# First context's keys and values of a cross attention, computed at the end of the stage before and left in PSUM

## The reference, cut to what matters

```python
x = x + _L1_ffn_ref(_layernorm(x), ...)              # stage 5: 8 experts, top 2, and a shared one
x = x + _L2_xattn_ref(_layernorm(x), ctx, ctx, ...)  # stage 6

def _L2_xattn_ref(Q, K, V, Wq, bq, Wk, bk, Wv, bv, Wo, bo):
    q = (Q @ Wq + bq) / T          # 16 heads of 16
    k = K @ Wk + bk                # K = V = the context
    v = V @ Wv + bv
    attn = softmax(einsum(q, k))
    return einsum(attn, v) @ Wo + bo
```

## Time and profile before

| | us |
|---|---|
| median of 3 runs | 1916.7 (1915.62 to 1917.58) |
| the profiled execution, its own time | 1916.3 |
| its span, first to last instruction | 1914.5 |
| TensorE busy | 1792.7 (94%) |
| VectorE busy | 1049.4 (55%) |
| ScalarE busy | 847.6 (44%) |
| GpSimd busy | 555.5 (29%) |
| mean granted TensorE clock | 0.979 |

### The profile page before, as it was taken

One profiled execution on the slowest core, in us unless ns is written; L12 is line 12 of the kernel. 1 busy time (PEld: TensorE's weight loads), 2 busy tenths in 40 slices (PEclk: granted clock), 3 DMA queues, 4 the chain that ended last, 5 costly groups with the idle time before them and its releaser, 6 DMA issues.

```text
span 1914.5 us, 42986 instructions
## 1 busy us (share of the span) xinstructions
PE 1792.7 (94%) x16790; PEld 1384.6 (72%) x16790; DVE 1049.4 (55%) x2665; ACT 847.6 (44%) x2411; POOL 555.5 (29%) x596
## 2 busy tenths in 40 slices
PE   8999889999999989899999989999799899998998
PEld 6886569844766756699999967777544577766787
DVE  7787752252366438875555545556755555447411
ACT  6664541232266344334333335555511566635332
POOL 4441133100254203301222113332202465514242
PEclk9999889999999999999999999999999999998899
DMA  4221069570124110051899642111011455300397
GB/s 150 53 62 43 13 243 324 192 237 29 26 49 121 37 56 3 25 202 64 306 330 335 246 135 85 48 50 60 4 56 60 111 155 154 100 1 2 125 347 251
DMA packets 88303, 234.02 MB, mean 122 GB/s; under 512 B 10176, under 2 KB 45664, under 8 KB 81600
## 3 DMA queue, kind: packets, MB, share of 16 engines
q1 hardware_dynamic: 78416, 210.61, 33.0%
q0 software_dynamic: 5664, 15.47, 2.5%
q10 hardware_dynamic: 4048, 5.52, 0.9%
HBM read 216.35 MB, written 12.07 MB: 119 GB/s over the span
## 4 chain that ended last, share of the span: by engine, by line
PE 75%; DVE 11%; DMA 5%; issue 4%; ACT 3%; POOL 1%; SPq 0%; ACTq 0%; POOLq 0%; PEldq 0%; DVEq 0%; PEld 0%
PE PS L1137 15%; PE PS L1606 6%; PE PS L1148 5%; PE PS L3682 3%; PE PS L3502 3%; PE PS L3186 3%; PE PS L3707 3%; PE PS L3194 3%; PE PS L2402 2%; PE PS L2459 2%; PE PS L2761 2%; PE PS L2443 2%; PE PS L3219 2%; DMA l1x_probsT<-in_ctx_dram 2%; PE PS L2473 1%
## 5 line engine op out<-in xcount | busy, mean ns | idle before, releaser
L2361 POOL TENSOR_TENSOR l1x_probs<-l1x_probs,l1x_total 128x512 f32<-128x512 f32 x64 | 68.4, 1070 | 208.7 <-DVE l1x_total L2609 208.6
L1606 PE MATMUL PS<-weights,l0x_ctxT 128*128 128x256 f32 x512 | 121.0, 387 | 0.0
L1137 PE MATMUL PS<-l1f_xT,l1f_slot 128*128 128x128 f32 x1024 | 117.0, 275 | 0.0
L1137 PEld LDWEIGHTS PS<-l1f_xT,l1f_slot 128*128 128x128 f32 x1024 | 115.7, 192 | 0.1
L1606 PEld LDWEIGHTS PS<-weights,l0x_ctxT 128*128 128x128 f32 x512 | 94.6, 191 | 14.8 <-issue 2.1
L3156 POOL TENSOR_TENSOR l2x_probs<-l2x_probs,l2x_total 128x512 f32<-128x512 f32 x64 | 65.0, 1038 | 129.7 <-DVE l2x_total L3352 129.7
L95 PE MATMUL PS<-consts 128*128 128x256 f32 x320 | 81.8, 401 | 1.2
L1264 DVE SCALAR_TENSOR_TENSOR l1f_product<-PS,l1f_slot,l1f_side 128x128 f32<-128x128 f32 x128 | 36.0, 344 | 65.9 <-ACT l1f_side L1220 65.9
L3682 PE MATMUL PS<-l3x_keysT,l3x_QW 128*128 128x289 f32 x256 | 69.4, 415 | 1.7 <-issue 1.7
L95 PEld LDWEIGHTS PS<-consts 128*128 128x128 f32 x320 | 61.7, 201 | 12.3 <-issue 4.4
L1090 POOL DMA_INDIRECT l1f_out_dram<-l1f_out,l1f_sort_target_row x23 | 22.7, 986 | 159.5 <-DVE l1f_out L1247 159.5
(11 more groups left out here) (661 smaller groups left out, 4583.7 us busy)
## 6 DMA issues: line engine op xcount, KB each, us to landing
l1f_slot<-in_experts_up_dram SPq DMA_DIRECT2D x16, 2056.0 KB, 9.9
weights<-in_experts_up_dram SPq DMA_DIRECT2D x8, 2056.0 KB, 10.2
l0f_slot<-in_experts_up_dram SPq DMA_DIRECT2D x15, 1024.0 KB, 7.9
weights<-in_experts_down_dram SPq DMA_DIRECT2D x21, 640.0 KB, 5.3
l1f_slot<-in_experts_down_dram SPq DMA_DIRECT2D x16, 640.0 KB, 4.5
l0x_ctxT<-in_ctxT_dram SPq DMA_DIRECT2D x32, 257.0 KB, 2.6
l2x_ctxT<-in_ctxT_dram SPq DMA_DIRECT2D x32, 257.0 KB, 2.7
l3x_ctxT<-in_ctxT_dram SPq DMA_DIRECT2D x32, 257.0 KB, 2.7
```

The costliest lines, as they stand in the source:

```text
L1137: done = nc.tensor.matmul(PS[:, bank + a, m * P:(m + 1) * P], mat[:, c, m * P:(m + 1) * P], x, start=(c == 0), stop=(c == 1))
L1606: last = nc.tensor.matmul(PS[:, 2 * (b % 2) + k, half * D:(half + 1) * D], ctxT[b % SLOTS][:, c, half * P:(half + 1) * P], kw[:, c, k * D: ...
L2361: nc.gpsimd.tensor_tensor(p, p, bcast(total[b % 2][:, 2 * n:2 * n + 2], 2, KEYS), ALU.mult).then_inc(probs_done, 1)
```

## The change

`SortedExperts.tensor` gets a hook `at_end(n)`, called with 0 where `keep_busy(5, 5)` stood and with 1 where `keep_busy(5, 12)` stood. Stage 5 uses it for the keys (n = 0) and the values (n = 1) of sequence 0 of stage 6, from a copy of context 0 that its SP program loads into a free part of `weights[0]`; behind the values stand 8 keep-busy matmuls in bank 3. Stage 11 passes a hook that keeps its 12 matmuls as they were. The results stay in banks 6, 4 and 5; two semaphores that outlive the stage, `first_keys` and `first_values`, tell stage 6 that they are there. In stage 6 `keys_values(0)` is gone, all counts of `k_done` and `v_done` are lower by one sequence, `ctxT` takes 1 and 2 on entry, and the flip of half 0 has no matmul ahead and its one behind in bank 7.

```diff
+        self.first_context_in, self.first_keys, self.first_values = self.sem("first_context_in"), self.sem("first_keys"), self.sem("first_values")
+        self.first_context = self.weights[0][:, 2640:2640 + C * CTX].rearrange("p (c k) -> p c k", c=C)
@@ SortedExperts.tensor
         def finish():
-            if self.kind == "swiglu":
-                self.core.keep_busy(5, 5)
+            at_end(0)
             down(*divmod(self.N - 1, RING), False)
 
         self.over(pe, lambda: S or flip_rows(0, 0), turn, finish)
         if self.K == 2:
-            self.core.keep_busy(5, 12)
+            at_end(1)
             self.sum_pairs(pe)
@@ l1_feed_forward, sync
             load_next(sp)
+            sp.dma_start(core.first_context, core.dram["ctxT"][0]).then_inc(core.first_context_in, 16)
             ex.load(sp, core.H, norm.wait_rows)
@@ l1_feed_forward, tensor
-            ex.tensor(pe, core.HT, between)
+            next_weights = core.arena(6)
+            next_weights.take(C, D)
+            wk, wv = next_weights.take(C, D), next_weights.take(C, D)
+
+            def at_end(n):
+                if n == 0:
+                    pe.wait_ge(core.weights_in[6], 16)
+                    pe.wait_ge(core.first_context_in, 16)
+                    for o in (1, 0):
+                        for c in range(C):
+                            last = nc.tensor.matmul(PS[:, 4 + 2 * o, 0:CTX], wk[:, c, o * P:(o + 1) * P], core.first_context[:, c, :], start=(c == 0), stop=(c == 1))
+                        last.then_inc(core.first_keys, 1)
+                else:
+                    for half in range(2):
+                        for c in range(C):
+                            last = nc.tensor.matmul(PS[:, 5, half * D:(half + 1) * D], core.first_context[:, c, half * P:(half + 1) * P], wv[:, c, :], start=(c == 0), stop=(c == 1))
+                    last.then_inc(core.first_values, 1)
+                    core.keep_busy(3, 8)
+
+            ex.tensor(pe, core.HT, between, at_end)
@@ l2_cross, sync
-            for b in range(2):
-                sp.dma_start(ctxT[b][:], core.dram["ctxT"][b]).then_inc(ctx_in[b], 16)
+            for b in range(1, 3):
+                sp.dma_start(ctxT[b % 2][:], core.dram["ctxT"][b]).then_inc(ctx_in[b % 2], 16)
...
             for b in range(1, B):
-                if b > 1:
-                    sp.wait_ge(k_done, 2 * (b - 2) + 2)
-                    sp.wait_ge(v_done, b - 1)
+                if b > 2:
+                    sp.wait_ge(k_done, 2 * (b - 2))
+                    sp.wait_ge(v_done, b - 2)
                     sp.dma_start(ctxT[b % 2][:], core.dram["ctxT"][b]).then_inc(ctx_in[b % 2], 16)
@@ l2_cross, tensor
-            flip.tensor(pe, 0, idle=(4, 1, 1))
+            flip.tensor(pe, 0, idle=(7, 0, 1))
...
-                pe.wait_ge(ctx_in[b % 2], 16 * (b // 2 + 1))
+                pe.wait_ge(ctx_in[b % 2], 16 * ((b + 1) // 2))
...
-            keys_values(0)
@@ l2_cross, scalar: copy_keys
-                    act.wait_ge(k_done, 2 * b + n + 1)
+                    act.wait_ge(*((k_done, 2 * b + n - 1) if b else (core.first_keys, n + 1)))
@@ l2_cross, vector: copy_values
-                dve.wait_ge(v_done, b + 1)
+                dve.wait_ge(*((v_done, b) if b else (core.first_values, 1)))
@@ l3_feed_forward, tensor
-            ex.tensor(pe, core.HT)
+            ex.tensor(pe, core.HT, at_end=lambda n: core.keep_busy(5, 12 * n))
```

More of the change, by code:

```diff
@@ L1103, in move_rows, with tensor @@
             store(i)
-    def tensor(self, pe, xT, between=lambda n: None):
+    def tensor(self, pe, xT, between=lambda n: None, at_end=lambda n: None):
         nc, PS, S, U = self.core.nc, self.core.PS, self.S, self.units
```

## The result

The changed kernel takes 1910.35 us, the median of 20 executions (1902.57 to 1917.77), beside 1915.21 us for the kernel before in the same comparison (20 executions, 1908.24 to 1922.2). The ratio is 0.9973 with a 95% interval of 0.9961 to 0.9984: 0.27% faster. The forecast was 1913.7 us, its range 1911.4 to 1916.4. The direction was right and the size was not: some 5 us instead of 3.0. One execution of the kernel before, of 2996.02 us at a granted clock of 0.555, fell among the later runs and is left out of every ratio and mean. The profiled execution has a span of 1910.5 us, against 1914.5.

The account below looks back on a forecast made before the run. TensorE was taken to bound the seam and the stage 6 loop. Removed work of 3.47 us less 0.23 of waiting less 0.24 of cold start saves 3.00, all else 0: 1913.7 us, range 1911.4 to 1916.4.

Parts of the forecast that it names:

- What is taken away: Ahead of `sim(0)` in stage 6: removing `keys_values(0)` takes 3.47 us off TensorE's chain, the most the edit can bring.
- what is late next: Behind the queries of half 1: values 1 wait 0.23 us for VectorE's copy of V; the saving is 3.00 us.
- the cold start: At values 1: a block of eight records behind a wait takes 1.97 us instead of 1.73, costing 0.24 us.
- The sum by the rule of the Trainium skill: At values 1: if weight loads are pulled past the wait, the saving is 3.24 us; the forecast kept 3.00.
- The broadcast of V_last: The copy of values 0 waits for the first part of `V_last`, with at least 4.9 us to spare; cost 0.
- the end of stage 5: Around the last `down`: eight records replace ten ahead, VectorE still decides; cost 0, bounds -0.1 and +0.1 us.
- the flip: Last transposes of stage 5: the matmul ahead is dropped, but ScalarE's fourth row sets their start; cost 0.
- SP's queue: In stage 5 one more issue (0.34 us) delays the store of the rows, with 27 and 49 us of cover; cost 0.
- The sum against the median: Whole kernel: 3.0 us off the profiled 1916.3 gives 1913.3; the median lies 0.4 above, so 1913.7 us.
- "So what is saved ahead of `sim(0)` arrives at the end of stage 6 in full": The stage 6 loop is bound by TensorE, so the saving passes through undiminished if first steps keep their distances.
- a larger saving: Later stages: the shift leaves one low-clock stretch (1.67 us) fewer, saving 4.7 us, time 1912.0; chance 0.15.
- Slower, by a low clock in `sum_pairs`: In `sum_pairs`, with fewer keep-busy matmuls, the clock is granted at 0.50, costing some 7 us, time 1920.8; chance 0.08.

Follow-up runs that it names:

- The kernel with 8 matmuls put back: Changed kernel with 8 keep-busy matmuls where keys and values 0 stood in stage 6; ratio 1.0002 to the kernel before, mean 1915.68 us.
- the three kernels with work put back: Changed kernel with 4, 8 or 16 keep-busy matmuls where keys and values 0 stood; ratios to the kernel before 0.9994, 1.0002 and 1.0019.
- one idle matmul more: Kernel before with one keep-busy matmul (0.43 us) added ahead of keys and values 0, run twice; ratios 1.001 and 0.9998, mean 1914.89 us.
- the early copy: Changed kernel with VectorE's copy of values 0 moved ahead of its query copies of half 1, run twice; ratios 0.9979 and 0.9983 to the kernel before.
- the changed kernel with the wait filled: Changed kernel with 6 keep-busy matmuls in TensorE's wait ahead of the queries of half 1; ratio 0.9987 to the kernel before, mean 1913.70 us.

## Why the prediction was wrong

- **What is taken away, what is late next.** Right. 3.00 us forecast, 3.14 and 3.15 measured. VectorE's copy of V did release values 1. The wait and the cold start cost 0.33 us, not 0.47. The wait was sized rightly, 0.22 us. The cold start was not: 0.10 instead of 0.24. The forecast took a length of the timeline (1.97 us, to the end of the last record) less one of the chain (1.73 us, to where the next block takes over); in the timeline a block in the stream has 1.89. V was also ready some 0.09 us sooner, as its copy overlaps the one ahead of it by 0.08 us, and TensorE began 0.05 us behind it, not 0.14. With the 4.22 us from the end of the queries to `sim(0)` the trace is 0.15 us under the forecast 4.37. The sum by the rule of the Trainium skill (TensorE: Matmul & The Clock Gate, "Step-by-step: what each phase is for"), read as a pull of weight loads past the wait, was 3.24; in the trace the loads rested behind the wait and the block took 1.99 us, so that reading doesn't hold here, though 3.15 us lies nearer to its sum than to 3.00, as the cold start that it leaves out is so short.
- **The broadcast of V_last, the end of stage 5, the flip, SP's queue.** Right, all at nothing. VectorE went from its query copies to the copy of V without a wait for `V_last`. The kernel with 8 matmuls put back has all of these edits and the time of before. The cover of SP's queue was read wrongly: by the earlier trace rows it is 29.7 us to SP's next issue (810.79 to 840.51) and 57 us to the first reader, not 27 and 49. The cost stays 0.
- **The sum against the median.** The first part of the miss. The base was 1916.7, a median of three, and it was taken as known to 0.7 us; 160 executions have a mean of 1915.7 and a median of 1915.6. I took the three runs' spread of 2.0 us for the scatter. It is 14 us from the lowest to the highest of 20, with a standard deviation of 3. That is 1.1 us of the 3.4 by which the forecast time is off, and it made the range too narrow. In the comparison of the result the kernel before has 1915.21: the forecast saving of 3.0 us from there would have been inside the range, and so would the measured saving of 4.9 us from 1916.7. It took both misses to leave it.
- **"So what is saved ahead of `sim(0)` arrives at the end of stage 6 in full".** It did, as the loop has the same length in all profiles, but the step stopped there and counted everything behind as unchanged. This is the second part: the changed kernel is 2.0 +- 0.5 us below what its seam gives (2.3 +- 0.7 by the first 32 executions), and the cause of these 2.0 us is open. It stands among the rivals as "a larger saving", with 4.7 us, 1912.0 us and 0.15. Its sign was right and its chance far too small, because I held that a shift by 3 us could only gain or lose a low stretch by luck. Measured, a saving of 4.9 us or more comes back in every set of the changed kernel. Whether a low stretch fewer makes it, as that rival has it, is not shown.
- **Slower, by a low clock in `sum_pairs`.** Not seen: the granted clock was 1.00 from 1104 to 1124 us, the rest ahead of `sum_pairs` 1.48 us, and in none of the 18 profiles does the clock fall in the 60 us ahead of the queries of half 1. What the Trainium skill (TensorE: Matmul & The Clock Gate, "What's actually happening") calls the default did not come back at this place; no run here shows how many keep-busy records could go before it does.

What stays open is what makes the 2.0 us. Shown is that they come back in every set, and, by the three kernels with work put back, that they don't come from the end of stage 5, the flip or the transfers. Shown is also that the length of the part behind the seam moves by up to 10 us with no edit in it, and that TensorE's busy time there moves with the time at 1.2 GHz at an equal count of records. Only argued is that the kernel before begins its later stages at an offset to the low stretches that costs some 4 us, and that a shift by 0.3 or 0.4 us leaves it.

For it: the two profiles of the kernel before have 44.4 and 48.9 us at 1.2 GHz in this part and the four of the changed kernel 37.5 to 41.6; one idle matmul more gave the shorter part in both profiles; and the early copy, 0.33 us the other way, had the longer part in one of two. Against it: with one idle matmul more the kernel before was no faster than its own kernel before; the kernels with 8 and 16 put back, one to one in the mean, had short parts in their single profiles; and the mean granted clock over all executions is 0.9784 for the kernel before (140) and 0.9790 for the changed one (50), 0.0006 +- 0.0003 apart. At 1.24 to 1.97 us for 0.001 that is an estimate of 0.7 to 1.1 us, half of the 2.0 at most, and itself only two standard errors from nothing. Some hundred executions of each, with the clock by stage, would decide it.

## What to carry to other kernels

Work moved from where TensorE is the bound into its wait for something else saves its length less what the next engine then makes it wait; read that engine's queue, with the cold start of the block behind the wait, and the sum comes out to 0.2 us. Take all lengths of such a sum from one view: a block's length in the timeline and its share of the chain differ by 0.16 us here. In the 18 profiles the clock of this kernel fell 13 to 20 times, for 74 to 95 us in all, and its time scatters by far more than such an edit is worth: find the scatter from many executions, not from three, give the range that width, compare each kernel with executions of the other from the same set, and compare traces stage by stage. A local gain of 3.15 us came out as 5.1 us on the whole, and 4.8 us (the changed kernel with the wait filled) as 2.0, so an edit at the 0.1% level has to be judged on means of dozens of executions.

## What the runs showed that I had not expected

- A wait of 2.84 us ahead of the queries of half 1 was followed by the 1.2 GHz level in 14 of the 15 profiles with this wait: in the one with 8 matmuls put back the same queries took 3.67 instead of 5.37 us, with no edit ahead of them.
- Filling that wait gave its 1.70 us at the spot in all three kernels, and nothing measurable in the whole.
- The changed kernel with the wait filled was 3.1 +- 1.1 us slower than without.
- The kernel before, with one idle matmul added, could not be told from it in time (ratios 1.001 and 0.9998), and yet in both its profiles the part behind the seam was 3 to 5 us shorter than in the two of the kernel without it.
